# Gate and up products of the first chunks of three dense feed-forward layers, placed inside the router that weighs them

## The reference

```python
router_probs = softmax(x @ gate_weight.T)
router_top_value, router_indices = top_k(router_probs, 8)
routing_weights = router_top_value / sum(router_top_value)
# the 4 weaker experts of a token go to a similar one of its 4 stronger, if similar enough
combine = sum(one_hot(rerouted_indices, E) * routing_weights[..., None], axis=1)
for wgu, wd, cw in experts:
    g, u = split(x @ wgu.T)
    y = y + (silu(g) * u) @ wd.T * cw[:, None]
```

## Time and profile before

| | us |
|---|---|
| median of 3 runs | 2070.52 |
| lowest and highest | 2068.43, 2072.03 |
| the profiled execution | 2077.71 |
| its span, first to last instruction | 2075.9 |
| first and last TensorE start of the gate and up products, L0 | 330.9 and 500.4 |
| the same, L1 | 704.1 and 945.7 |
| the same, L2 | 1523.3 and 1681.9 |

### The profile page before, as it was taken

How to read it: one execution, slowest core, us unless ns; L and a number is a source line. 1 busy time by engine, 2 the same in 40 slices (tenths; PEclk the granted TensorE clock), 3 DMA queues, 4 the chain that set the end, 5 groups by cost and what they waited for, 6 DMA issues and landing times. The chain is left out here.

```text
span 2075.9 us, 26147 instructions
## 1 busy us (share of the span) xinstructions
PE 1637.5 (79%) x8443; PEld 1015.1 (49%) x8484; DVE 1184.1 (57%) x2685; ACT 813.9 (39%) x1839; POOL 721.5 (35%) x1442
## 2 busy tenths in 40 slices
PE   7688878998785599994488888888679989636762
PEld 5322234555554355553156566566545565425551
DVE  5799972223554533325778888888832255562235
ACT  3888862111322111113377777777621112312220
POOL 0022210000100479301578888888300000036662
PEclk9755558999786799997799999999989988757786
DMA  1288761110403022111100000000011100335535
GB/s 69 54 164 158 159 140 37 38 38 16 162 1 125 23 103 72 52 55 42 41 1 1 1 1 1 1 1 1 24 26 38 38 30 1 121 132 197 196 119 218
DMA packets 174489, 139.99 MB, mean 67 GB/s; under 512 B 142065, under 2 KB 154993, under 8 KB 170658
## 3 DMA queue, kind: packets, MB, share of 16 engines
q1 hardware_dynamic: 164898, 113.31, 19.4%
q0 software_dynamic: 7104, 23.60, 3.5%
q10 hardware_dynamic: 2368, 1.61, 0.2%
HBM read 85.43 MB, written 19.50 MB: 51 GB/s over the span
## 5 line engine op out<-in xcount | busy, mean ns | idle before, releaser
L304 PE MATMUL l1e_gu<-x_normT,l1e_w 128*128 128x512 f32 x384 | 169.6, 595 | 0.2 <-DVE l1e_h L350 0.2
L1881 ACT ACTIVATE l0m_pf<-l0m_s,l0m_bias,l0x_sq 128x1024 int16<-128x1024 f32 x128 | 154.0, 1203 | 38.8 <-POOL l0m_bias L1813 38.8
L1423 PE MATMUL l2x_pr<-l_w,l2x_xq 128*128 128x512 bf16 x538 | 135.4, 388 | 42.6 <-ACT credits L42 40.7
L1907 DVE TENSOR_REDUCE l0m_mx<-l0m_s 128x1 f32<-128x1024 f32 x128 | 156.0, 1220 | 21.5 <-PE l0m_s L1823 20.1
L1823 PE MATMUL l0m_s<-l0x_kT,l0x_qT 48*128 48x512 bf16 x256 | 124.9, 615 | 36.9 <-ACT l0m_pf L1881 32.9
L1552 DVE TENSOR_SCALAR l2x_raw<-l2x_raw,l2x_mv,l2x_rs 128x128 f32<-128x128 f32 x384 | 128.3, 394 | 20.5 <-POOL l2x_rs L1402 20.0
L348 DVE TENSOR_TENSOR l1e_h<-l1e_sil,l1e_gu 128x512 f32<-128x512 f32 x48 | 33.0, 688 | 164.6 <-ACT l1e_sil L333 156.5
L1813 POOL TENSOR_SCALAR l0m_bias<-l0m_mx,l0x_nsq 128x1 f32<-128x1 f32 x128 | 46.4, 362 | 227.5 <-DVE l0m_mx L1907 226.1
L304 PE MATMUL l0e_gu<-x_normT,l0e_w 128*128 128x512 f32 x272 | 120.7, 597 | 0.0
L304 PEld LDWEIGHTS l1e_gu<-x_normT,l1e_w 128*128 128x128 f32 x384 | 73.3, 191 | 83.4 <-issue 81.1
L304 PE MATMUL l2e_gu<-x_normT,l2e_w 128*128 128x512 f32 x256 | 113.1, 595 | 0.0
(11 more groups left out here) (527 smaller groups left out, 3773.3 us busy)
## 6 DMA issues: line engine op xcount, KB each, us to landing
l3m_w<-in_l_moe SPq DMA_DIRECT2D x16, 1280.0 KB
l1e_w<-in_l_ffn SPq DMA_DIRECT2D x24, 384.0 KB, 3.0
l_rows<-zero_row SPq DMA_DIRECT2D x8, 1024.0 KB, 11.1
l_w<-l_rows SPq DMA_DIRECT2D x8, 1024.0 KB, 12.5
l0e_w<-in_l_ffn SPq DMA_DIRECT2D x17, 384.0 KB
l2e_w<-in_l_ffn SPq DMA_DIRECT2D x16, 384.0 KB, 3.1
l1e_route<-l_route SPq DMA_DIRECT2D x8, 512.0 KB
l2q_wps<-in_l_wp SPq DMA_DIRECT2D x16, 256.0 KB, 2.7
```

The lines of the kernel that those rows point to most:

```text
L304: last = nc.tensor.matmul(gu[half][:, m, :], w[:, slot, (2 * k + m) * P:(2 * k + m + 1) * P], pg.xnT[:, k, half * HALF:(half + 1) * HALF], ...
L1423: last = nc.tensor.matmul(flat(pr[t % 2][:]), src[:, k, tokens], pg.l2_w3[:, part, k, at:at + W], start=(k == 0 and part == 0), stop=(k == ...
L1881: nc.scalar.activation(pf[:, n % 4, :], s_ps[n % 3][:], ACT.Exp, scale=sq[:, b, h:h + 1], bias=bias[:, n % 4:n % 4 + 1], accum_out=sm[:, b ...
L1907: nc.vector.tensor_reduce(mx[:, n % 4:n % 4 + 1], s_ps[n % 3][:], AX, ALU.max).then_inc(s["maxed"], 1)
```

## The change

`router` and `experts` become one block, `ffn_block`. What it does:

- `ahead` chunks (3 in L0 and L2, 4 in L1) are computed up to the product of silu and up before the route is known: `early = 2 * ahead` halves. TensorE does them with `fill_pe` inside the router: 2 behind the logits in L0, 3 in L2; in L1 2 behind the logits and 4 behind the products with the similarities. The rest (4, 3 and 2) follow the transposes of `cw`.
- For an early half ScalarE copies up out of PSUM (`upc`) and takes the silu of gate; GpSimd multiplies the two into `h`. The later halves are multiplied by VectorE from PSUM, as before. VectorE multiplies with the route when this has come (`weigh`), and TensorE runs `ahead` chunks ahead of the down products instead of one.
- There are `ahead + 2` weight slots instead of 3, all first loaded in `norm`, and `ahead + 1` buffers of `h`. A slot is loaded anew `ahead + 2` chunks later.
- The router's PSUM tiles are views of the banks of `y`. The zeroing products are gone: the first product into each bank starts it. `cwT` lies in the last buffer of `h`; in L1 the one-hot rows and `route` share the attention's context buffer, and other router buffers lie in `xn`.
- All loops are written out, without `Fori`. SyncE issues the reads of `route` in all layers, behind the store of `cwT`; in L1 the first two tiles together.
- `l2_split` starts on GpSimd behind the eight early multiplications. Semaphores are cleared behind `l1x` and `l2f` instead of `l1f` and `l3x`.

The diff, cut to its core:

```diff
+def ffn_block(pg, name, E, rows, scratch, weights, n_chunks, ahead, tiles, segments, pool_last, allocate, pool_prog, act_prog, vector_prog, pe_prog,
+              sp_prog=None):
...
+    SW, SH = ahead + 2, ahead + 1
+    w, w_in = pg.expert_w, pg.expert_w_in
...
+        h = st.enter_context(nc.sbuf_tensor(f"{name}e_h", [P, SH, T], F32))
+        r.cwT = h[0:rows, ahead, :]
+        sil = st.enter_context(nc.sbuf_tensor(f"{name}e_sil", [P, 2, HALF], F32))
+        upc = st.enter_context(nc.sbuf_tensor(f"{name}e_up", [P, 2, HALF], F32))
+        if name == "l1":
+            route = pg.ctxt[:].rearrange("p (a b) d -> p a (b d)", a=2)
+        else:
+            route = st.enter_context(nc.sbuf_tensor(f"{name}e_route", [P, 2, T], F32))[:]
+        y = st.enter_context(nc.psum_tensor(f"{name}e_y", [P, B, D], F32))
+        gu = [st.enter_context(nc.psum_tensor(f"{name}e_gu{i}", [P, 2, HALF], F32)) for i in range(2)]
+
+
+        def bank(i):
+            return y[:, 2 * i:2 * i + 2, :].rearrange("p a d -> p (a d)")
+        r.lg = bank(0).rearrange("p (b e) -> p b e", e=64)
+        r.tp = r.ot = [bank(1), bank(2)]
+        r.rows = [bank(3), bank(0)]
+        allocate(r, sb)
         block = st.enter_context(nc.Block())
+
+
+        early = 2 * ahead
...
+        def route_of(c):
+            if moving:
+                turn = c // 3
+                return turn % 2, turn // 2
+            at = 0
+            for j, count in enumerate(segments):
+                at += count
+                if c < at:
+                    return j, 0
 
         @block.sync
         def _(sp):
+            def spread(at, n):
+                return scratch[at:at + n, :].unsqueeze(1).to_broadcast([n, P // n, T])
+
+            def turn_in(turn):
+                if turn >= 2:
+                    sp.wait_ge(routed, 2 * 3 * (turn - 1))
+                sp.dma_start(route[:, turn % 2, :], spread(turn * tiles, tiles)).then_inc(route_in[turn % 2], 16)
+
             if sp_prog:
                 sp_prog(r, sp)
             sp.wait_ge(r.kept, 2)
-            sp.dma_start(scratch, r.cwT[:]).then_inc(r.stored, 16)
+            sp.dma_start(scratch, r.cwT).then_inc(r.stored, 16)
             sp.wait_ge(r.stored, 16)
+            if moving:
+                turn_in(0)
+                turn_in(1)
+            else:
+                for j, (at, n) in enumerate(tiles):
+                    sp.dma_start(route[:, j, :], spread(at, n)).then_inc(route_in[j], 16)
+            for c in range(SW, n_chunks):
+                if moving and (c - SW + 1) % 3 == 0:
+                    turn_in((c - SW + 1) // 3 + 1)
+                sp.wait_ge(downs, c - SW + 1)
+                sp.dma_start(w[:, c % SW, :], weights[c]).then_inc(w_in[c % SW], 16)
...
             pool_prog(r, pool)
+            for n in range(early):
+                pool.wait_ge(copied, n + 1)
+                pool.wait_ge(silu_done, n + 1)
+                nc.gpsimd.tensor_tensor(h[:, n // 2, cols(n)], sil[:, n % 2, :], upc[:, n % 2, :], ALU.mult).then_inc(early_done, 1)
+            if pool_last:
+                pool_last(pg, pool)
...
+            def up(n):
+                c, half = divmod(n, 2)
+                pe.wait_ge(w_in[c % SW], 16 * (c // SW) + 16)
+                if n >= 2 and n - 2 < early:
+                    pe.wait_ge(copied, n - 1)
+                    pe.wait_ge(silu_done, n - 1)
+                elif n >= 2:
+                    pe.wait_ge(mul_done, n - 2 - early + 1)
+                for m in range(2):
+                    for k in range(KD):
+                        last = nc.tensor.matmul(gu[half][:, m, :], w[:, c % SW, (2 * k + m) * P:(2 * k + m + 1) * P],
+                                                pg.xnT[:, k, cols(n)], start=(k == 0), stop=(k == KD - 1))
+                last.then_inc(gu_done, 1)
+
+            def down(c):
+                pe.wait_ge(routed, 2 * c + 2)
+                for t in range(B):
+                    last = nc.tensor.matmul(y[:, t, :], h[:, c % SH, t * P:(t + 1) * P], w[:, c % SW, WG:CHUNK],
+                                            start=(c == 0 and t % 2 == 0), stop=False, skip_group_check=True)
+                    if c == n_chunks - 1 and t % 2:
+                        last.then_inc(y_done, 1)
+                if c < n_chunks - 1:
+                    last.then_inc(downs, 1)
+
+            filled = [0]
+
+            def fill(n):
+                for _ in range(n):
+                    up(filled[0])
+                    filled[0] += 1
+            r.fill_pe = fill
...
+            pe_prog(r, pe)
             pe.wait_ge(r.route, 1)
             for g in range(2):
                 for i in range(4):
                     last = nc.tensor.transpose(r.tp[g][0:rows, i * P:(i + 1) * P], r.cw[:, 4 * g + i, :], pg.ident[:])
                 last.then_inc(r.turned, 1)
+            fill(early - filled[0])
+            pe.wait_ge(r.kept, 2)
+            for c in range(n_chunks):
+                if c + ahead < n_chunks:
+                    up(2 * (c + ahead))
+                    up(2 * (c + ahead) + 1)
+                down(c)
...
+            def silu(n):
+                act.wait_ge(gu_done, n + 1)
+                if 2 <= n < early + 2:
+                    act.wait_ge(early_done, n - 1)
+                if n < early:
+                    s.activation(upc[:, n % 2, :], gu[n % 2][:, 1, :], ACT.Copy).then_inc(copied, 1)
+                s.activation(sil[:, n % 2, :], gu[n % 2][:, 0, :], ACT.Silu).then_inc(silu_done, 1)
+
+            def fill(n):
+                for _ in range(n):
+                    silu(filled[0])
+                    filled[0] += 1
+            r.fill_act = fill
...
+            for n in range(filled[0], 2 * n_chunks):
+                silu(n)
...
+            def multiply(n):
+                c = n // 2
+                dve.wait_ge(silu_done, n + 1)
+                if n % 2 == 0 and c >= SH:
+                    dve.wait_ge(downs, c - SH + 1)
+                v.tensor_tensor(h[:, c % SH, cols(n)], sil[:, n % 2, :], gu[n % 2][:, 1, :], ALU.mult).then_inc(mul_done, 1)
+
+            def weigh(c):
+                buf, use = route_of(c)
+                dve.wait_ge(route_in[buf], 16 * use + 16)
+                for n in (2 * c, 2 * c + 1):
+                    if n < early:
+                        dve.wait_ge(early_done, n + 1)
+                    else:
+                        dve.wait_ge(mul_done, n - early + 1)
+                    v.tensor_tensor(h[:, c % SH, cols(n)], h[:, c % SH, cols(n)], route[:, buf, cols(n)], ALU.mult).then_inc(routed, 1)
+
+            for c in range(n_chunks):
+                weigh(c)
+                if c + ahead < n_chunks:
+                    multiply(2 * (c + ahead))
+                    multiply(2 * (c + ahead) + 1)
...
-def router_l0(pg, scratch):
+def router_l0(pg, scratch, *args):
...
+        r.fill_act(2)
+
+    def pe_prog(r, pe):
+        r.fill_pe(2)
...
+def router_l1(pg, scratch, *args):
...
+        r.fill_pe(2)
         pe.wait_ge(r.vec_done, 2)
...
             last.then_inc(r.pe_done, 1)
+        r.fill_pe(4)
 
     def act_prog(r, act):
         exp_scalar(r, act)
+        r.fill_act(2)
         for g in range(2):
             act.wait_ge(r.pe_done, g + 1)
-            nc.scalar.activation(r.oneT[:, g * HALF:(g + 1) * HALF], r.ot[g][:], ACT.Copy).then_inc(r.act_done, 1)
+            nc.scalar.activation(r.oneT[:, g * HALF:(g + 1) * HALF], r.ot[g], ACT.Copy).then_inc(r.act_done, 1)
+        r.fill_act(4)
...
+def router_l2(pg, scratch, *args):
...
+        r.fill_act(3)
+
+    def pe_prog(r, pe):
+        r.fill_pe(3)
...
-            "l0f": lambda: ffn("l0", 9, router_l0, 17, 3, 3, [(8, 1), (0, 8)], [6, 11]),
+            "l0f": lambda: ffn("l0", 9, router_l0, 17, 3, [(8, 1), (0, 8)], [6, 11], None),
...
-            "l1f": lambda: ffn("l1", 32, router_l1, 24, 3, 6, 4, None, l2_split),
+            "l1f": lambda: ffn("l1", 32, router_l1, 24, 4, 4, None, l2_split),
...
-            if name in ("l1f", "l3x"):
+            if name in ("l1x", "l2f"):
                 clear_semaphores(pg)
```

More of the change, by code:

```diff
@@ L548, in allocate @@
         r.bj = sb("bj", [P, 5, B, S])
-        r.ot = [psum(f"ot{i}", [P, HALF]) for i in range(2)]
-        r.rows = [psum(f"rows{i}", [P, HALF]) for i in range(2)]
     def pool_prog(r, pool):
@@ L590, in vector_prog @@
         dve.wait_ge(r.consts, 1)
-        one = r.one[:].rearrange("p b k e -> p (b k) e")
+        one = r.one.rearrange("p b k e -> p (b k) e")
         v.tensor_tensor(one, r.io[:].unsqueeze(1).to_broadcast([P, B * K, E]),
@@ L2234, in ffn @@
             route = scratch(f"{name}_route", rows)
-            n_chunks, slots, body, *rest = args
+            n_chunks, ahead, *rest = args
+            slots = ahead + 2
             with ExitStack() as early:
@@ L2255, in ffn @@
                 norm(pg, f"{name}n", pg.x, preload)
-                router_of(pg, route)
```

(2 more changed lines are left out.)

185 lines of the change are left out of this document (29 added, 156 removed).

## The result

The changed kernel takes **2019.68 us** in the median of four runs (2017.57 to 2022.93), beside 2070.1 for the kernel before: a ratio of 0.9762 (95% interval 0.9745 to 0.978), 50.4 us less. The profiled execution took 2022.93 us.

What follows compares the result with a forecast made beforehand. TensorE was taken to bound the dense loops, idling in the routers ahead of them. Gains of 11.3 + 15.0 + 25.9 = 52.2 us turn the profiled 2077.71 into 2025.5 and the median 2070.52 into 2018, range 2011 to 2030.

Steps and rivals of the forecast that it cites:

- The bound, and halves off the end one by one: TensorE bounds the dense loops; each half done in a router's stretch takes 3.43 us off the end, at most 69.7 us.
- From the profiled execution to the median: Whole kernel: the median lies 7.2 us under the profiled execution, outside the three stages, so 2025.5 becomes 2018.
- Layer 0: Layer 0's router stretch: 12.53 us less 1.0 for transposes and 0.2 for the clock, gain 11.3 us.
- the cold start: First halves behind layer 0's logits: the low clock costs 1.7 us after the change against 1.5 before.
- Layer 2: Layer 2's router stretch: 16.48 us less 1.0 and 0.5, gain 15.0 us.
- Layer 1: Layer 1's router: gain 25.9 us, with 1.1 us VectorE delay against 1 us gained, and a thin margin for the route.
- The free edits: ScalarE copies, more weight slots loaded in the norm, later weight splitting and moved semaphore clears cost nothing.
- the stretched chain: Rival in layer 1: all eight GpSimd multiplications lie in VectorE's chain, 8.5 us, 7.4 more than taken: 2025.5; chance 0.11.
- The late route: Rival: layer 1's two reads share queues, TensorE stands 7 us before the first down product: 2025; chance 0.09.
- The low clock: Rival: the seven halves behind the logits take 6.86 us each, 19 us in all over three layers: 2037; chance 0.07.
- Starving code: Rival in the written-out loops: instruction fetch holds each chunk; at 1.2 us per chunk 2086, slower than before; chance 0.03.
- it doesn't do what it says: Rival: early halves only push the router back; just block boundaries and the loops' cold starts are won: about 2054; chance 0.03.

Runs made afterwards that it cites:

- e1: Changed kernel with no early half inside the routers, all behind the transposes of cw: 2051.38 us beside 2071.8 for the kernel before, ratio 0.9901.
- e3: Changed kernel with all eight early halves of layer 1 ahead of the transposes of cw (six behind the similarities, not four): 2016.54 us, ratio 0.9737.
- e8: Changed kernel, L0 logits laced and three halves behind, L1 five halves behind similarities and GpSimd's fifth early product waiting for cw: 1996.46 us (second chip), ratio 0.9737.
- e9: e8 with GpSimd's splitting of the next attention's weights in L1 waiting until chunk 0 is multiplied with the route: 2011.11 us (third chip), ratio 0.9713.
- e4: Changed kernel with 512-column products laced between logits products, two halves in L0 (every four), one in L2 (every eight): 2025.35 us, ratio 0.9763.
- e7: Changed kernel with only L0's logits laced with two halves, and three halves instead of two behind them: 1999.46 us (second chip), ratio 0.9742.
- e10: Same kernel as e8, run on the third chip beside e9: 2014.11 us, ratio 0.9731 to the kernel before.
- e2: Changed kernel with GpSimd's early multiplications replaced by a memset of the same buffer: 2017.85 us, ratio 0.9741.
- e6: Changed kernel with GpSimd's fifth early product in L1 waiting until cw is done: 1999.08 us (second chip), ratio 0.9752.

## Why the prediction was right

2018 was predicted, in 2011 to 2030, and 2019.68 came. Point by point:

- **The bound, and halves off the end one by one**: right. In all three layers the first gate product follows the logits without idle time, no down product behind it waits, and e1 shows both parts of the gain, the boundary (12 us by the stages, 20 by whole times) and the filling (38 and 30).
- **From the profiled execution to the median**: right. I took it that the 7.2 us between them did not lie in the stages; 6.1 us lie behind L2's, in unchanged code.
- **Layer 0, 11.3 predicted, 10.5 measured.** The failed term is the cold start, which I let become 0.2 us dearer (1.7 against 1.5). It cost 2.3 us after and 1.3 before (15.22 us for four halves, 13.90 when warm), 1.0 dearer; 0.2 us too much before came from taking the start of ScalarE's step for the end of the half. The logits took 0.3 more (4.88 against 4.55), which no term held. Some 0.3 us came back, since the transposes held TensorE for 0.9 us (327.95 to 328.82) where 1.0 was assumed and the rows overlap a little. The route was multiplied in at 337.7, weighed at about 340, 11.7 us before the down product.
- **Layer 2, 15.0 predicted, 14.2 measured.** Again the clock, 0.5 us dearer by my terms (1.5 against 1.0): the first three halves took 12.89 us, 2.4 above the warm 10.46, and before it cost 0.8 (14.67 against 13.90). The first down product came 35.3 us after the start of the logits, where 35.0 was worked out.
- **Layer 1, 25.9 predicted, 25.6 measured**, with an error inside. I let one GpSimd product meet one two-input multiplication, for 1.06 us. Two met one each, and a 128x512 product takes 1.27, not half of the 2.12 of the earlier trace rows; I had passed over the short steps as too short to matter, and one of 0.22 us waited out a whole product. Contention was 2.0 us and not 1.1. The sign named for this rival, a multiplication far over 2.29 us, came at 3.34. The first product behind the similarities came 1.1 us earlier, as taken. Measured from the logits' end the transposes come after 34.6 us, before 33.7. The first down product is 57.6 us behind the start of the logits, worked out as 57.1; the spare time of the route was 1.9 us, in the 1.5 to 2 given. That the gain is off by only 0.3 us is partly luck: the transposes took 1.7 us and not 1.9, the clock 0.6 and not 0.7, and the kernel before lost 1.2 us at the loop's start and not 1.1.
- **The free edits**: free. Chunks stay at 10.32 us, and the splitting of the weights ends at 847.99, no later than in the earlier trace rows. One came near to a price: the router's four small loads of similarities (`sim`) are issued behind the larger preload and landed after 13.1 us instead of 9.4. GpSimd had them after 15.8 us instead of 10.9, at 663.46, and TensorE needed them at 664.79. In e3 they were what TensorE waited for last, at no cost yet (17.47 us after the logits' start, 17.44 in the changed kernel).

Of the rivals, the stretched chain was half true in kind and a quarter in size (2.0 of 8.5 us). The late route did not come in the changed kernel: two reads together, issued at 693.40, were there at 701.73, 8.3 us after, as one alone was. It came in e3, e8 and e9, where TensorE had fewer halves left behind the transposes. The low clock stayed for one burst's start, not for seven halves. Starving code shows in no chunk. That it doesn't do what it says is refuted by e1, which is what that rival describes, and which landed at 2051.38 where it was priced at 2054: the changed kernel is some 30 us under that.

## What to carry to other kernels

A serial stretch such as a router can be hidden behind the product work that follows it, up to the point where its result is needed, and the gain can be counted in pieces of that work. Then count three things with it: the cold clock behind every stretch of thin products or idle time; the wait that replaces the filled one (keep enough work behind the result to cover its way through memory); and, on GpSimd, every two-input step that can fall onto a VectorE step of the critical chain, the short ones too. Work that nobody waits for, such as the weight splitting here, should start behind the chain's last step. In the changed kernel it did not reach the route multiplications (1.31 us), and the wait would have won nothing there. Once a fifth half was filled in (e8), it did, and that single wait took 3.4 us off the stage (269.6 to 266.2) where filling further had taken 1.2 (270.8 to 269.6).

## What the runs showed of the hardware

- In these traces the granted clock fell to 1.2 GHz in L0 while TensorE was busy without a gap on products of 9 columns, and the dense products behind paid 1.8 to 2.4 us (9.29, 8.87 and 12.89 us where 7.03, 7.03 and 10.46 are warm). With a 512-column product after every four, the clock stayed where it was at entry: 1.00 in e4, e7 and e9, 0.50 in e10 until ten us later. With one after every eight it fell in L2 of e4 (stage 179.5 us).
- A wait of 4 us ahead of dense work cost 1.8 us more by the clock (5.41 and 5.38 us in e3, e8 and e10 against 3.62), one of 2.04 us only 0.1 (e9). A wait removed can so give back less than its length: 1.1 us of 2.0 in e2 and e6, 1.2 of 3.0 in e3.
- L2's logits took 4.72 us in the changed kernel's profile and 6.96 in e1's, by the same code; where they are long the stage is 175 us and not 172.8 (e2, e3, e6, e8; e1 had long ones too). The stretch from L1's stage to L2's is shorter where the stage is longer (544.9 to 545.1 against 546.1 to 549.5). What sets it was not tried.
- A `tensor_scalar` of 128x8 with one input in SBUF, 0.16 us elsewhere, took 0.98 beside GpSimd's product in L2 (at 1481.22). Two-input steps are not the only ones that meet it. The other way round, a GpSimd `tensor_scalar` of 128x1024 (2.86 us) left two-input multiplications that began 0.96 us or more into it at their length (1.31, 1.28 and 1.29 us for two at 701.73, 747.68 and 758.00).
